# Attention probabilities' PSUM copy moved from VectorE to ScalarE, and LayerNorm done over 1024 tokens at once, in a transformer layer on 8 cores

## The reference

```python
HQ, HKV, HD, WIN = (16, 4, 128, 512)

def attn(x):                                   # x: (2, 4096, 2048)
    q = (x @ Wq) ; k = (x @ Wk) ; v = (x @ Wv) # 16 query heads, 4 key/value heads
    scores = q @ k.T / 128                     # banded: each query sees 512 keys
    probs = softmax(where(valid, scores, neg))
    return (probs @ v) @ Wo

def ffn(x):                                    # weights int32 0..255, H=2048, I=8192
    W = (w.astype(float32) - 128.0) * scale[:, None]
    return (silu(x @ Wg.T) * (x @ Wu.T)) @ Wd.T

def _layernorm(x, axis=-1, eps=1e-5):
    return (x - mean(x)) / sqrt(var(x) + eps)

x = _layernorm(x + attn(x))
x = _layernorm(x + ffn(x))
```

## Time and profile before

| what | value |
|---|---|
| median of 2 runs | 2512.61 us (2511.86 to 2513.36) |
| the profiled execution's own time | 2511.3 us |
| its span, core 6, the slowest | 2509.7 us (cores 2494.6 to 2509.7) |
| PE busy | 2108.2 us, 84% |
| PEld (weight loads) busy | 942.6 us, 38% |
| DVE busy | 568.2 us, 23% |
| ACT busy | 280.8 us, 11% |
| POOL busy | 113.1 us, 5% |
| DMA | 147.66 MB, mean 59 GB/s |
| mean granted TensorE clock, core 6 | 0.891 |

### The profile page before, as it was taken

The page is one execution under the profiler, slowest core; times in us unless marked ns, Lnnn a source line. Parts: engine busy times, 40 slices in busy tenths (PEclk is TensorE's granted clock), DMA queues, the critical chain, the costliest instruction groups (busy, mean ns, idle before and its releaser), DMA issues.

```text
span 2509.7 us, 24037 instructions; the slowest of 8 cores (2494.6 to 2509.7 us)
## 1 busy us (share of the span) xinstructions
PE 2108.2 (84%) x9616; PEld 942.6 (38%) x9616; DVE 568.2 (23%) x998; ACT 280.8 (11%) x513; POOL 113.1 (5%) x217
## 2 busy tenths in 40 slices
PE   0689767776895569999999999899999999999941
PEld 0234344444340034444443444344444443444200
DVE  0111188888113311011010000000110100000033
ACT  0000033333003320010100000010101010000121
POOL 1000000000000000000000000000000000000000
PEclk9999855555897789999999999999999999999975
DMA  9343200000340034343432333343434333333003
GB/s 223 47 68 67 55 1 1 1 1 1 67 68 0 0 67 80 72 84 68 84 68 53 64 67 67 57 75 71 84 68 84 68 67 61 61 65 66 17 0 134
DMA packets 31919, 147.66 MB, mean 59 GB/s; under 512 B 3906, under 2 KB 6084, under 8 KB 27076
## 3 DMA queue, kind: packets, MB, share of 16 engines
q0 software_dynamic: 30800, 127.94, 28.6%
q1 hardware_dynamic: 1012, 18.20, 2.1%
HBM read 265.66 MB, written 8.39 MB: 109 GB/s over the span
## 4 chain that ended last, share of the span: by engine, by line
PE 81%; DVE 8%; another core or an unknown queue 3%; issue 3%; DMA 2%; ACT 2%; DVEq 0%; POOL 0%; ACTq 0%; POOLq 0%; SPq 0%
PE psD L682 18%; PE psG L582 18%; PE psU L590 18%; PE psW L394 5%; PE psQ L195 4%; PE pT L294 3%; DVE ab L331 3%; PE psD L678 3%; PE pv L307 3%; PE psS L428 2%; PE psS L452 2%; DVE S_sb L517 2%; PE psH L648 1%; PE psQ L204 1%
## 5 line engine op out<-in xcount | busy, mean ns | idle before, releaser
L582 PE MATMUL psG<-ab 128*128 128x512 bf16 x2048 | 456.3, 381 | 44.0 <-DMA ab<-wu_is 44.0
L682 PE MATMUL psD<-ab 128*128 128x512 bf16 x2048 | 454.7, 380 | 0.0
L590 PE MATMUL psU<-ab 128*128 128x512 bf16 x2048 | 452.5, 379 | 0.0
L582 PEld LDWEIGHTS psG<-ab 128*128 128x128 bf16 x2048 | 201.3, 98 | 289.9 <-issue 51.0
L682 PEld LDWEIGHTS psD<-ab 128*128 128x128 bf16 x2048 | 195.4, 98 | 276.4 <-issue 50.8
L590 PEld LDWEIGHTS psU<-ab 128*128 128x128 bf16 x2048 | 200.3, 98 | 241.8
L602 DVE SCALAR_TENSOR_TENSOR ab<-psU,scl_sb,sq_sb 128x512 bf16<-128x512 f32 x128 | 90.2, 747 | 824.1 <-PE psU L590 824.1
L617 ACT ACTIVATE sq_sb<-psG,scl_sb 128x512 f32<-128x512 f32 x128 | 88.0, 687 | 774.3 <-PE psG L582 774.3
L294 PE MATMUL pT<-Dm_sb,ab 128*128 128x128 bf16 x640 | 88.5, 303 | 96.7 <-DVE sums_sb L334 90.8
L692 DVE SCALAR_TENSOR_TENSOR S_sb<-psD,scl_sb,S_sb 128x1024 f32<-128x1024 f32 x32 | 41.1, 1284 | 479.8 <-PE psD L682 479.8
L294 PEld LDWEIGHTS pT<-Dm_sb,ab 128*128 128x128 bf16 x640 | 58.1, 131 | 167.4 <-issue 167.4
(11 more groups left out here) (66 smaller groups left out, 990.7 us busy)
## 6 DMA issues: line engine op xcount, KB each, us to landing
ab<-wg_is POOLq DMA_DIRECT2D x64, 512.0 KB, 5.0
ab<-wu_is POOLq DMA_DIRECT2D x64, 512.0 KB, 7.0
ab<-wd_os POOLq DMA_DIRECT2D x32, 1024.0 KB, 7.9
ab<-wq_os POOLq DMA_DIRECT2D x16, 512.0 KB, 5.0
ab<-wo_os POOLq DMA_DIRECT2D x16, 512.0 KB, 5.0
ab<-x_all POOLq DMA_DIRECT2D x1, 6144.0 KB, 67.8
ab<-wv_ks POOLq DMA_DIRECT2D x16, 128.0 KB, 69.9
ab<-wk_os POOLq DMA_DIRECT2D x4, 512.0 KB, 5.6
```

Source lines behind the costliest of these rows:

```text
L582: last = t.matmul(psG[i % 2][:, 512 * tt:512 * tt + 512], abv(wgu_o + 4096 * (i % 2) + 128 * k, 128), abv(y1_o + 1024 * k + 512 * tt, 512) ...
L590: last = t.matmul(psU[i % 2][:, 512 * tt:512 * tt + 512], abv(wgu_o + 4096 * (i % 2) + 2048 + 128 * k, 128), abv(y1_o + 1024 * k + 512 * t ...
L682: last = t.matmul(psD[o % 2][:, 512 * tt:512 * tt + 512], abv(wd_o + 4096 * (o % 2) + 128 * i, 128), abv(h_o + 1024 * i + 512 * tt, 512), ...
```

## The change

There are two parts.

**Attention.** The pT copy leaves VectorE and goes to ScalarE, as `s.copy`, with the same shape and type. ScalarE's stream is now, for each step n: exponential of n, pT copy of n-2. The waits of TensorE that named `vv` for this copy name `ss`, and the numbers of the `ss` counts are worked out ahead for both kinds of instruction. All else stays: buffers, steps, the other waits.

**LayerNorm.** The loop over the halves is gone and there is one barrier instead of two. The statistics rows and `psB1`, `psB2` are 1024 wide (two PSUM banks each). All 32 sum matmuls run in a row, then the 32 squares and their matmuls. The addition of eps on ScalarE is gone: two more matmuls add D x eps to `psS2` from a new constant row `eps_row`, loaded with the other constants. The variance, its reciprocal and the root are now formed in place in PSUM, and a copy of the root to SBUF is added before the four spreading matmuls. The blocks are multiplied, subtracted and copied 1024 columns at a time.

```diff
-                        t.wait_ge(vv, c_pTe[m])
+                        t.wait_ge(ss, c_pTe[m])
...
-                    if 0 <= n - 2 < NIT:
-                        m = n - 2
-                        v.wait_ge(tm, c_tD[m])
-                        c_pTe[m] = inc(v.tensor_copy(abv(pT_o + 640 * (m % 2), 640), pTp[:, :]), "vv")
...
+                for n in range(NIT + 2):
+                    if n < NIT:
+                        s.wait_ge(vv, c_msk[n])
+                        if n >= 3:
+                            s.wait_ge(tm, c_tD[n - 3])
+                        got = inc(
+                            s.activation(abv(probs_o + 640 * (n % 3), 640), scs[n % 2][:, :], AF.Exp,
...
+                    if 0 <= n - 2 < NIT:
+                        m = n - 2
+                        s.wait_ge(tm, c_tD[m])
+                        got = inc(s.copy(abv(pT_o + 640 * (m % 2), 640), pTp[:, :]), "ss")
```

```diff
+                    for tt in range(2):
+                        inc(t.matmul(psS2[:1, 512 * tt:512 * tt + 512], onr_sb[:1, :1],
+                                     eps_sb[:1, :], start=False, stop=True), "tm")
...
+                    inc(v.tensor_scalar(psM, psS1[:1, :], 1.0 / D, None, ALU.mult), "vv")
...
+                    inc(s.activation(psQ2, psM, AF.Square), "ss")
...
+                    inc(v.scalar_tensor_tensor(psS2[:1, :], psS2[:1, :], 1.0 / D,
+                                               psQ2, ALU.mult, ALU.subtract), "vv")
+                    v.wait_ge(vv, cnt["vv"])
+                    inc(v.reciprocal(psS2[:1, :], psS2[:1, :]), "vv")
...
+                    inc(s.activation(psS2[:1, :], psS2[:1, :], AF.Sqrt), "ss")
...
+                    inc(v.tensor_tensor(psQ2, psM, psS2[:1, :], ALU.mult), "vv")
+                    v.wait_ge(vv, cnt["vv"])
+                    inc(v.tensor_copy(psM, psS2[:1, :]), "vv")
...
+                    for k in range(KC):
+                        sl = S_sb[:, 1024 * k:1024 * k + 1024]
+                        inc(v.tensor_tensor(sl, sl, psB1[:, :], ALU.mult), "vv")
```

More of the change, by code:

```diff
@@ L417, in emit_ln, with _ @@
             li = _ln_id[0]
[L418 to L426, removed]
+            with nc.psum_tensor(f"psS1_{li}", [1, 1024], F32) as psS1, \
+                 nc.psum_tensor(f"psS2_{li}", [1, 1024], F32) as psS2, \
+                 nc.psum_tensor(f"psB1_{li}", [128, 1024], F32) as psB1, \
+                 nc.psum_tensor(f"psB2_{li}", [128, 1024], F32) as psB2:
+                @block.tensor
+                def _(t):
+                    t.wait_ge(sq, p0_sq)
+                    last = None
+                    for tt in range(2):
@@ L427, in _ @@
                         for k in range(KC):
[L428 removed]
+                            last = t.matmul(psS1[:1, 512 * tt:512 * tt + 512], onc_sb[:, :1],
                                             S_sb[:, 1024 * k + 512 * tt:1024 * k + 512 * tt + 512],
                                             start=(k == 0), stop=(k == KC - 1))
[L431 to L433 removed]
@@ L434, in emit_ln, with _ @@
-                    ss0_sq = cnt["ss"]
-                    c_sq = [ss0_sq + k + 1 for k in range(KC)]
+                    inc(last, "tm")
+                tm0_sq = cnt["tm"]
+                c_smm = [tm0_sq + j + 1 for j in range(2 * KC)]
+                ss0_sq = cnt["ss"]
+                c_sq = [ss0_sq + j + 1 for j in range(2 * KC)]
+                @block.scalar
+                def _(s):
+                    for j in range(2 * KC):
+                        tt, k = j // KC, j % KC
+                        if j >= 2:
+                            s.wait_ge(tm, c_smm[j - 2])
+                        got = inc(
+                            s.activation(sq_sb[:, 512 * (j % 2):512 * (j % 2) + 512],
+                                         S_sb[:, 1024 * k + 512 * tt:1024 * k + 512 * tt + 512],
+                                         AF.Square), "ss")
+                        assert got == c_sq[j]
@@ new lines, in _ @@
+                @block.tensor
+                def _(t):
+                    for j in range(2 * KC):
+                        tt, k = j // KC, j % KC
+                        t.wait_ge(ss, c_sq[j])
+                        got = t.matmul(psS2[:1, 512 * tt:512 * tt + 512], onc_sb[:, :1],
+                                       sq_sb[:, 512 * (j % 2):512 * (j % 2) + 512],
+                                       start=(k == 0), stop=False)
+                        assert inc(got, "tm") == c_smm[j]
+                    for tt in range(2):
+                        inc(t.matmul(psS2[:1, 512 * tt:512 * tt + 512], onr_sb[:1, :1],
+                                     eps_sb[:1, :], start=False, stop=True), "tm")
@@ new lines, in emit_ln, with _ @@
+                tm_bc = cnt["tm"]
+                ln_done = [None] * KC
+                @block.vector
+                def _(v, ln_done=ln_done):
+                    v.wait_ge(tm, tm_bc)
+                    for k in range(KC):
+                        sl = S_sb[:, 1024 * k:1024 * k + 1024]
+                        inc(v.tensor_tensor(sl, sl, psB1[:, :], ALU.mult), "vv")
+                    mid = cnt["vv"]
+                    v.wait_ge(vv, mid)
+                    for k in range(KC):
+                        sl = S_sb[:, 1024 * k:1024 * k + 1024]
+                        ln_done[k] = inc(v.tensor_tensor(sl, sl, psB2[:, :], ALU.subtract), "vv")
@@ L448, in _ @@
[L448 to L467, removed]
-                    c2 = cnt["ss"]
@@ L524, in emit_ln @@
[L524 to L532 removed]
+                            s.wait_ge(vv, ln_done[k])
@@ L534, in build_nc @@
+                            inc(s.copy(abv(write_bf16_to + 1024 * k, 1024),
+                                       S_sb[:, 1024 * k:1024 * k + 1024]), "ss")
+                barrier()
         emit_ln(write_bf16_to=y1_o)
```

130 lines of the change are left out of this document (54 added, 76 removed).

## The result

The changed kernel takes 2479.47 us (median of 7 runs), the kernel before 2512.44 in the same comparison: a ratio of 0.9868, with a 95% interval from 0.9855 to 0.9880. It is faster by 1.3%, clear of the interval, and within the 2% that was called "no change". The forecast was 2479.6. One of the 7 runs, of 2532.3 us, had the cores of one die at a lower granted clock; runs of this kind are left out of the ratios, and of the medians of the experiments.

A forecast was written before the change was run, and what follows sets the result against it. Attention was taken as bound by a 2.50 us loop, with one of 2.41 next. Gains of 12.2 us there and 20.8 in LayerNorm, 33.0 off 2511.3, plus 1.3 to the median, gave 2479.6 us, range 2473 to 2486.

The forecast's parts named there:

- Two loops: Steady attention: pT copy, transposition, PV product, output copy, 2.50 us; mask, exponential, reciprocal, diagonal, next mask, 2.41, comes next.
- The exponential's second wait: Attention: the exponential's wait on the transposition of item n-3, said to add 0.06 us per item.
- 122 x 0.09: Attention: the 122 items left each take 2.41 us instead of 2.50, 11.0 us gained.
- statistics with eps: LayerNorm: sum and square passes of both halves, 57.8 us, plus 1.7 for four eps passes: 59.5, 1.0 gained.
- chain on one partition: LayerNorm: mean, variance, reciprocal, root and spreading matmuls, once at 1024 wide: 24.5 us against 31.4, 6.9 gained.
- multiply and subtract: LayerNorm: 32 operations of 1024 columns at 1.14 us each, 36.8 us against 38.8, 2.0 gained.
- copies' end and next stage: End of LayerNorm: last copy ends 0.4 us later, one barrier goes; 0.6 gained in LayerNorm 1, about 0.4 in LayerNorm 2.
- Rival E: LayerNorm: eight removed table loads worth 2.66 us each, not 1.28, so 11 us more gained: 2468.6; chance 0.02.
- A: Attention: the pT copy on ScalarE becomes the bound, over 0.83 us; at 1.0 attention gains nothing: 2491; chance 0.11.
- B: Attention: the 0.06 us of the exponential's wait vanishes, 2.35 per item, 7.3 more gained: 2472; chance 0.09.
- C: Attention: ScalarE reloads tables between exponential and copy, 194 us more, 2686 in total; chance 0.04.
- D: LayerNorm: doubled widths just double the costs and eps passes cost 0.96 us each: 2490; chance 0.06.

The follow-up runs named there:

- the table of four cases: pT copy on VectorE or ScalarE, reciprocal and diagonal in their step or one later: 2.50 and 2.50 us per item on VectorE, 2.42 and 1.83 on ScalarE.
- the ten pieces: The changed kernel with the pT copy of 640 columns cut into ten copies of 64: 2498.6 us.
- the kernel with both loops cut: The changed kernel with VectorE's reciprocal and diagonal done one step later, behind the next mask: 2402.8 us.

## Why the prediction was right, point by point

**The bound.** Two loops, 2.50 and 2.41 us, one a little behind the other: right. The chain after the change, the 2.41 in the timeline, and the table of four cases all show it. The busy share of VectorE, 88% before, would have suggested a gain of up to 0.8 us an item; 0.08 came.

**The exponential's second wait.** Read from two pairs of items as 0.06; taking it away gave 0.06. Right.

**The pT copy on ScalarE.** Taken at 0.70, measured 0.683. The limit from which it would bound was put at 0.83; it is 0.93 in the copy's own duration, as the copy starts 0.10 before the end of the read. The step was mis-sized by this, on the side that did no harm.

**The gain in attention.** 12.2 forecast, 10.7 measured. The term that was mis-sized is 122 x 0.09. Mask 2 to mask 127 gained 9.7 us where 11.0 were expected. Most intervals are 2.40 or 2.41, but ten are 2.59 to 2.69, about every 16 items, and the average is 2.42. The prediction took the bare period. In eight of these, exactly 16 items apart, the mask starts 0.45 us after the diagonal's start (up to 0.48) instead of 0.27, with nothing waited for. In the other two (2.68 and 2.69) it is the exponential that starts late, 1.25 after the mask's start instead of 0.98. What holds the engines there wasn't tried and stays open. The drain at the end gave 1.1, expected 1.2.

**LayerNorm**, by its terms in LayerNorm 1:

| term | forecast | measured |
|---|---|---|
| statistics with eps | 59.5 | 59.9 |
| chain on one partition | 24.5 | 24.0 |
| multiply and subtract | 36.8 | 36.5 |
| copies' end and next stage | 1.5 | 1.7 |

Forecast 20.8 us for both, measured 22.5. In LayerNorm 2 the three terms are 59.9, 24.0 and 36.5 again, so the chain came out 0.5 shorter in each. Besides, LayerNorm 2 took longer before than LayerNorm 1, whose halves the forecast used for both: its statistics took 60.8 (60.5 in the forecast) and its multiply and subtract 39.2 (38.8). The eps passes cost 0.43 each, as taken, and not 0.96. The loads that left the chain were worth 1.28 each: the load starts at 805.29, 0.08 after the mean has ended, and the square follows it at 806.58, so nothing of 1.38 us stands there. Rival E is out. The Trainium skill gives 2.66 us for every switch of sets, in "ScalarE: Activation LUTs", section "What ACT_TABLE_LOAD costs"; for these loads, with ScalarE idle before them, the trace has 1.28.

**The rivals.** A did not happen, and the ten pieces show at which size it would have. B did not happen until the wait was removed. C is out: one table load for 128 exponentials and 128 copies in one block. By the Trainium skill's rule on sets ("ScalarE: Activation LUTs", section "Table sets: the hidden batching unit") copy is in every set. The trace now agrees for the exponential's. D is out by the table above.

**The total** came out 0.1 us from the forecast, and that is luck. By the traces the gain is 31.8 us and not 33.0: 1.5 less than forecast in attention, 1.7 more in LayerNorm, 1.5 less in the feed-forward stage, whose own scatter is larger than that, and 0.1 more at the ends. The last 1.2 is made up by the step from the profiled execution to the median: the forecast added 1.3, as in the kernel before, while the profiled execution of the changed kernel is itself the median, 2479.47. An error of some 2 us in each part is what the method gave here.

## What to carry to other kernels

In a software pipeline, look for every loop from an item to the next and write down its length before moving work off the busiest engine: a copy of 0.82 us that left VectorE gave 0.08, since a second loop was only 0.09 shorter, while the same move with that loop cut gave 0.67, and 1.04 with ScalarE's order changed too, both with the help of TensorE's clock, which rose from 0.50 to 1.00. The first items of a stage, where the queues are still empty, show the length of the inner loops by themselves. And a wait costs time on such a loop even if what it waits for was done long ago; drop those that order on the same engine already implies.

## What was not expected of the hardware

TensorE's granted clock in attention was 0.50 throughout in the kernel before, from 309 to 625 us (one window in the earlier trace rows), with TensorE busy 42.0 of 60 us. In the changed kernel it averages about 0.6:

```profile
340.00:400.00 60.00, 39.08 (x295) 27.37 (x296) 38.56 (x99) 34.06 (x75) 0.00 (x0) 0.62 0.00 1
```

Its items come 3 to 4% closer together, and some run at 2.4 GHz (a transposition of 0.44 instead of 0.69 us). With 1.83 and 1.46 us per item the clock is at 1.00 throughout. The forecast did not speak of it, and for the changed kernel it made no difference, since TensorE isn't on the loop that bounds: of the 20 intervals with a fast transposition 17 are 2.40 or 2.41, as most others. For the kernel with both loops cut it decided between 1.80 and 2.19.

ScalarE's operation on 1024 elements of one partition takes 1.05 us from SBUF to SBUF (the square) and 0.97 from PSUM to PSUM (the root); no run has the same function at this width in both places. Copies of a few columns follow each other closely: five of 128 columns take 0.93 us together and ten of 64 take 1.24, where one of 640 takes 0.68.
